# Decoder block with three-pass fp32 matmuls: the last three pairs of heads go batch by batch, with each batch's cross attention beside the next batch's steps

## The reference, cut to what matters

```python
# x (4,512,512), ctx (4,512,256); 16 heads = 8 pairs
x = layernorm(x + gated_slot_attention(x, Wq, Wk, Wv, Wg, Ws, Wo))   # per head: q,k,s 64 wide, v,g 128 wide
    # p = exp(s - cumlogsumexp(s)), a scan over tokens for keys, softmax over 64 slots,
    # a scan for values, rms norm, silu(g) gate, then @ Wo (the sum over heads)
# cross attention, per batch; logits are the x just normalised
q = ctx @ Wq.T + bq ; k = ctx @ Wk.T + bk
att = softmax(q @ k.T)                      # 512 x 512, one batch
x = layernorm(x + x @ att.T)
# FFN: BitNet (8-bit rows, ternary weights), Hadamard transform over the 2048 hidden values
gate, up = bitlinear(x, w_gate), bitlinear(x, w_up)
x = layernorm(x + bitlinear(hadamard(silu(gate) * up), w_down))
```

## Time and profile before

| | |
|---|---|
| median of 3 runs | 1638.67 us (1638.44 to 1642.08) |
| profiled execution, its time | 1641.68 us |
| its span, first to last instruction | 1639.8 us |
| mean granted PE clock | 0.976 of full speed |
| PE busy | 1536.7 us, 94% |
| DVE busy | 1038.5 us, 63% |
| ACT, POOL busy | 630.7 us, 367.8 us |

### The profile page before, as it was taken

One profiled execution on the slowest core, in us unless ns is written; L12 is line 12 of the kernel. 1 busy time (PEld: TensorE's weight loads), 2 busy tenths in 40 slices (PEclk: granted clock), 3 DMA queues, 4 the chain that ended last, 5 costly groups with the idle time before them and its releaser, 6 DMA issues.

```text
span 1639.8 us, 23987 instructions
## 1 busy us (share of the span) xinstructions
PE 1536.7 (94%) x9570; PEld 1215.1 (74%) x9570; DVE 1038.5 (63%) x1982; ACT 630.7 (38%) x1213; POOL 367.8 (22%) x246
## 2 busy tenths in 40 slices
PE   6999999999999999999999999896969797999986
PEld 5888888888888888888888888785746455656663
DVE  4566556556655655665565566465667777778785
ACT  4332333233233323323332332222132646567663
POOL 1111002001100202433342343232011333233210
PEclk9999999999999999999999999997989899999998
DMA  7111012111101200211121120210040122334451
GB/s 249 49 55 42 27 33 65 40 39 57 41 27 33 65 14 26 66 57 41 52 71 53 52 65 33 71 52 20 7 167 1 58 84 89 97 104 142 142 167 58
DMA packets 88062, 106.99 MB, mean 65 GB/s; under 512 B 4496, under 2 KB 58896, under 8 KB 87568
## 3 DMA queue, kind: packets, MB, share of 16 engines
q1 hardware_dynamic: 84496, 99.17, 18.8%
q10 hardware_dynamic: 3456, 6.29, 1.0%
HBM read 78.19 MB, written 27.26 MB: 64 GB/s over the span
## 4 chain that ended last, share of the span: by engine, by line
PE 85%; DVE 8%; issue 2%; ACT 2%; DMA 1%; POOL 1%; SPq 0%; POOLq 0%; DVEq 0%; ACTq 0%
PE bank L393 18%; PE bank L395 17%; PE bank L394 17%; PE bank L604 5%; PE bank L502 3%; PE bank L640 3%; PE bank L488 2%; PE bank L438 2%; PE bank L464 2%; PE bank L619 2%; PE bank L447 2%; PE bank L510 2%; PE bank L452 2%; PE bank L459 1%; PE bank L496 1%
## 5 line engine op out<-in xcount | busy, mean ns | idle before, releaser
L393 PE MATMUL bank<-Wh,X 128*128 128x512 f32 x512 | 211.2, 412 | 0.0
L395 PE MATMUL bank<-Wh,X 128*128 128x512 f32 x512 | 200.9, 392 | 0.0
L394 PE MATMUL bank<-Wl,X 128*128 128x512 f32 x512 | 200.1, 391 | 0.0
L731 ACT ACTIVATE V<-bank 128x256 f32<-128x256 f32 x128 | 49.2, 384 | 369.2 <-PE bank L395 369.2
L393 PE MATMUL bank<-X,Wh 128*128 128x512 f32 x384 | 163.6, 426 | 15.7 <-DVE X L905 13.0
L1287 POOL TENSOR_TENSOR sm<-sm,half 128x8 f32<-128x8 f32 x32 | 52.7, 1646 | 501.1 <-DVE sm L1010 501.1
L395 PE MATMUL bank<-X,Wl 128*128 128x512 f32 x384 | 153.2, 399 | 0.0
L394 PE MATMUL bank<-X,Wh 128*128 128x512 f32 x384 | 152.4, 397 | 0.0
L604 PE MATMUL bank<-XT,W 128*128 128x512 bf16 x512 | 123.2, 384 | 12.5 <-DVE M L1158 3.9
L1277 POOL TENSOR_SCALAR RAW<-RAW 128x1024 f32<-128x1024 f32 x24 | 87.4, 3640 | 158.3 <-ACT RAW L709 158.2
L953 DVE SCALAR_TENSOR_TENSOR U<-U,bank 128x256 f32<-128x256 f32 x128 | 51.7, 404 | 96.2 <-ACT U L733 96.0
(11 more groups left out here) (188 smaller groups left out, 3240.3 us busy)
## 6 DMA issues: line engine op xcount, KB each, us to landing
z_scratch<-EV SPq DMA_DIRECT2D x64, 256.0 KB, 2.0
Z<-z_scratch SPq DMA_DIRECT2D x16, 1024.0 KB, 6.0
RAW<-wgT SPq DMA_DIRECT2D x16, 512.0 KB, 3.8
RAW<-wuT SPq DMA_DIRECT2D x16, 512.0 KB, 3.7
RAW<-wdT SPq DMA_DIRECT2D x16, 512.0 KB, 3.6
w_scratch<-BW ACTq DMA_DIRECT2D x24, 256.0 KB, 2.0
W<-w_scratch SPq DMA_DIRECT2D x3, 2048.0 KB, 12.3
RAW<-Wo SPq DMA_DIRECT2D x8, 512.0 KB, 3.6
```

The source lines that it names most:

```text
L393: engine.matmul(o, lh(c), rh(c), start=c == 0, stop=False)
L394: engine.matmul(o, lh(c), rl(c), start=False, stop=False)
L395: last = engine.matmul(o, ll(c), rh(c), start=False, stop=c == n - 1)
L731: engine.activation(V[:, par, i, :], bk[:, 0:256], ACT.Copy).then_inc(S["v_evac"], 1)
```

## The change

The list of (pair, batch) is now a table, `PAIRS`. Pairs 0 to 4 go as before; pairs 5, 6 and 7 go batch by batch, with the pairs in turn up and down (5, 6, 7, then 7, 6, 5), so the last step of one batch and the first of the next share their weights. Batches end with steps 22, 25, 28 and 31. There are 14 sets of weights instead of 8. The new sets are loaded behind the last use before them, in loops 18, 19, 20, 22, 23, 25, 26, 28 and 29 for Q, K, S, VG (before: 18, 22 and 26 in that stretch).

The stages of cross attention are placed by four tables, one for each batch. `PLACED` are 16 stages of a loop, so place 16 n + i is behind the i-th of them in loop n; 496 on are the seam's 22 places, 518 on the units from 4. Batch 0 stands in loops 25 to 28 (all but `x_turned` in 25 to 27), batch 1 in loops 27 to 29, batch 2 from loop 29 to the seam; batch 3's softmax is in the seam, its `centre` at unit 4, its `xm0` at unit 16 and its `x_turned` at unit 29. Between values and unit 0 stands no `xm` any more, and `y` of step 31 moves behind unit 3.

The FFN's weight pieces (`tern`) may stand three times a loop, and all are made by loop 24. Buffers move: the low part of the context goes to the back half of `X1h`, low parts of the attention to two tiles of their own, `M` is in two pieces. `W3` (made weights) comes back in halves of columns: gate and up for units 0 to 7 first, then the rest, then the down weights. `x_turned_out` of batches 0 to 2 waits for other things that held its tile.

```diff
-WEIGHT = {"Q": 0, "K": 1, "S": 2, "VG": 4, "WO": 5}
+PAIRS = [(hp, b) for hp in range(5) for b in range(NB)]
+PAIRS += [(hp, b) for b in range(NB) for hp in ((5, 6, 7), (7, 6, 5))[b % 2]]
+FIRST = [n for n in range(STEPS) if n == 0 or PAIRS[n][0] != PAIRS[n - 1][0]]
+LOAD = [sum(f <= n for f in FIRST) - 1 for n in range(STEPS)]
+LAST = [f - 1 for f in FIRST[1:]] + [STEPS - 1]
+ENDS = [max(n for n in range(STEPS) if PAIRS[n][1] == b) for b in range(NB)]
...
+STEP = ("keys", "q", "scores", "states", "load_x", "k", "ok", "s", "tern", "turn_ok", "turn_o", "vg0", "tern",
+        "turn_w", "vg1", "y", "weights", "vg2", "values", "vg3", "tern")
+def step_order(n, tasks):
...
+        if stage == "tern":
+            terns += 1
+            if n and terns in ((2,) if n + 1 in LAST else (1, 2, 3)):
...
+def new_weights(stage, n):
+    l = LOAD[n]
+    if n != LAST[l] or l + 1 == LOADS:
+        return []
+    return {"q": [("Q", l + 1)], "k": [("K", l + 1)], "s": [("S", l + 1)], "y": [("WO", l + 1)],
+            "vg3": [("VG", l + 1, 0), ("VG", l + 1, 1)]}.get(stage, [])
...
-            if n == STEPS - 2 and stage in BETWEEN:
-                yield from cross_place(0, BETWEEN[stage])
+            if stage in PLACED and n > 20:
+                yield from beside(len(PLACED) * n + PLACED.index(stage))
+SEAM = (("keys", 31), ("scores", 31), ("states", 31), ("turn_o", 30), ("ok", 31), ("y", 30), ("turn_ok", 31), None,
+        ("turn_w", 31), None, None, None, ("weights", 31), ("values", 31), None, None, ("turn_o", 31), ("unit", 0),
+        ("unit", 1), ("unit", 2), ("unit", 3), ("y", 31))
+PLACES = (
+    dict(ctx=400, centre=403, n1=406, qk=406, qk_out=407, x101=411, x101_out=412, x123=416, x123_out=417,
...
+    dict(ctx=500, qk=502, qk_out=503, energy=506, energy_out=507, att_scale=508, att01=510, att01_out=511,
+         att23=511, att23_out=512, centre=518, n1=521, x101=524, x101_out=525, x123=527, x123_out=528, xm0=530,
...
-                if no == len(pieces) - 6:
-
-                    sp.wait_ge(S["proj_vg"], 4 * (STEPS - 3))
+                if loop >= 22 and 0 not in placed:
+                    sp.wait_ge(S["proj_vg"], 4 * ENDS[0] + 4)
                     engine.dma_start(XW[:, 0], xWqT.rearrange("(c p) n -> p c n", p=128)).then_inc(S["xw_in"], 16)
                     engine.dma_start(XW[:, 1], xWkT.rearrange("(c p) n -> p c n", p=128)).then_inc(S["xw_in"], 16)
                     context(0)
+                if loop >= 27 and 1 not in placed:
+                    sp.wait_ge(S["ctx_lo"], 1)
+                    context(1)
...
-            for k in range(3):
-                engine.dma_start(W3[:, k, :], scratch[k]).then_inc(S[f"w3_in{k}"], 16)
+            for h in range(2):
+                for k in range(2):
+                    v = lambda a: a.rearrange("p (c n) -> p c n", c=4)[:, :, 1024 * h:1024 * h + 1024]
+                    engine.dma_start(v(W3[:, k, :]), v(scratch[k])).then_inc(S[f"w3_in{h}"], 16)
+            sp.wait_ge(S["w_lo_g"], 6 * (LOADS - 1))
+            engine.dma_start(W3[:, 2, :], scratch[2]).then_inc(S["w3_in2"], 16)
```

More of the change, by code:

```diff
@@ L1 @@
+import math
 import numpy as np
@@ L37, in attention_order @@
+PLACED = [stage for stage in STEP if stage not in ("scores", "load_x", "tern")]
 def attention_order():
-    for stage in ("q", "k", "s", "vg0", "vg1", "vg2", "vg3"):
+    for stage in OF_NEXT:
         yield stage, 0
     yield "load_x", 2
-    tern = iter(range(51))
+    tasks = list(range(52))
     for n in range(STEPS - 1):
[L45 to L56, removed]
-            if n == STEPS - 2 and stage in BETWEEN:
-                yield from cross_place(0, BETWEEN[stage])
@@ L62 @@
-FIRST = {"weights": (("ctx", 0), ("centre", 0)), "values": (("n1", 0),), "vg3": (("qk", 0),)}
-BETWEEN = {"keys": 1, "q": 2, "states": 3, "k": 4, "ok": 5, "s": 6, "turn_o": 7, "vg0": 8, "turn_w": 9, "vg1": 10, "y": 11,
-           "weights": 12, "vg2": 13, "values": 14, "vg3": 15}
-def seam_order():
[L69 to L75, removed]
+        for stage, m in step_order(n, tasks):
+            yield stage, m
+            if stage in PLACED and n > 20:
+                yield from beside(len(PLACED) * n + PLACED.index(stage))
@@ L80, in seam_order @@
             yield item
[L84 to L101, removed]
@@ L106, with cross_places, beside @@
+CROSS = set(PLACES[0])
+def cross_places():
+    at = {}
+    for b in range(NB):
+        for stage, place in PLACES[b].items():
+            at.setdefault(place, []).append((stage, b))
+    return at
+BESIDE = cross_places()
+def beside(place):
+    return BESIDE.get(place, ())
 TILE = (("scale", 5), ("round", 6), ("clamp", 7), ("turn_q_out", 9), ("add", 11), ("normal", 12), ("store", 12),
         ("turn_q", 8), ("down", 10))
-SEAM_UNITS = 7
 LAG = 23
@@ L141 @@
         *(stage for stage, _ in TILE)}
[L144 to L167, removed]
 SEMAPHORES = """
-const_in gw_in raw0_in raw1_in am_in og_in v_in u_in y_in0 y_in1 y_in2 y_in3 ctx_in xw_in xb_in w3_in0 w3_in1 w3_in2 w3_store out_done
+const_in vec_in raw0_in raw1_in am_in og_in v_in u_in y_in0 y_in1 y_in2 y_in3 ctx_in xw_in w3_in0 w3_in1 w3_in2 w3_store out_done
 vec_made hk_zero
@@ L1336, in gpsimd @@
                     attend(stage, n)
+                    for key in new_weights(stage, n):
+                        w_low(key)
         def sync(engine):
@@ L1351, in sync @@
             held = {}
-            for no, (key, where) in enumerate(pieces):
+            placed = set()
+            for no, (key, where, loop) in enumerate(pieces):
                 if no == 10:
```

217 lines of the change are left out of this document (135 added, 82 removed).

## The result

The changed kernel takes 1585.62 us (median of 4 runs, 1584.94 to 1586.57) against 1639.16 of the kernel before in the same comparison. The ratio is 0.9671, with a 95% interval of 0.9654 to 0.9687: 53.5 us faster. Predicted were 1579.5 us and a range of 1556 to 1622. The profiled execution took 1585.25 us, its span is 1583.1.

What follows compares the result with a forecast made beforehand. PE was taken as the bound, losing 90.4 us late to waits and lower clock. 1549.6 without loss plus 1, 12 and 18 gave a 1580.6 us span, so 1579.5 us forecast; range 1556 to 1622.

Steps and rivals of the forecast that it cites:

- The reachable loss and its source: Loops 28 to 30, step 31 and the units: 90.4 us lost to late cross-attention stages or late loads; without loss 1549.6.
- The forecast case: Whole kernel: most lost time comes back, 1579.5 us, own range 1556 to 1606; chance 72%.
- Weights, 1 us: Loops 18 to 29: six more weight sets are covered by other work, costing 1 us; bounds 0 and 79.
- rival 3: Nine loops with a weight set: slots starve PE, 8.8 us each, 1659 us, slower by 19; chance 5%.
- The late FFN piece, 8.8 us: Loop 28: no FFN piece is fetched there any more, so its 8.8 us loss is gone.
- Loops 25 to 30, 12 us: Cross attention of batches 0 to 2 beside the loops loses 2 us a loop, 12 in all; bounds 0 and 66.
- Step 31, 10 us: Step 31: DVE decides, with a root on POOL as last link before unit 0; 10 us lost.
- Units 0 to 22, 8 us: Units 0 to 22: 8 us lost for the start and for centre and n1 between h and gs.
- The signs: Trace readings named beforehand, such as step 31's keys at 1205 to 1220 us; wrong if loops 28 to 30 exceed 52.
- 1: Step 31 and the units: waits stay, 59.7 us lost as before, 1622 us (1621 as median); chance 10%.
- 2: Loops 25 to 30: DVE and POOL queues jam, batches 0 to 2 lose 21.9 us each, 1634 us; chance 10%.
- 4: Whole kernel: no effect, through mishaps that happen to sum to 60 us; chance 3%.

Runs made afterwards that it cites:

- Run 1: Changed kernel with the last pairs in order 5, 6, 7 for every batch: 17 weight sets instead of 14, last FFN pieces two loops later; 1587.24 us.
- Run 2: Kernel before, with SP's loads of the context and its weights three FFN pieces later; 1630.73 us, ratio 0.9945.
- run 8: Changed kernel without POOL's root of the attention output's mean square, so values differ; 1579.66 us against 1585.97 for the changed kernel on the same chip.
- a11_scale: Also run 11: a10_early with batch 0's scaling of exponentiated rows one place earlier on DVE, ahead of an instruction waiting for PE; 1580.63 us.
- run 6: Changed kernel with the splits of batch 3's context (ACT, POOL) one place earlier, 499 instead of 500; 1586.38 us.
- run 3: Changed kernel with batch 0's cross attention packed on places 426 to 444 instead of 400 to 444; 1597.38 us.
- a4_ring0: Changed kernel with batch 0's second x1 and its energy two places later and the halves of its att one place later; 1583.01 us.
- a9_norecip: Changed kernel with DVE's reciprocal of the running sums replaced by a short copy, so values differ; 1581.66 us, ratio 0.9644.
- a10_early: a4_ring0 with batch 0's row maxima on DVE one place earlier, ahead of DVE's step for ok; 1582.53 us, ratio 0.9652.

## Why the prediction was right

**The reachable loss and its source: right.** The end without any loss was put at 1549.6 us. The span came out 33.5 above it, where 31 were predicted. Of the 6.1 us between 1579.5 and 1585.62 the span makes 2.5; 3.4 come from taking off 3.0 us because the profiled execution of before was above its median, while the one of after is 0.4 under its own. The tail reads 86.98 us against 87.2. (The mark at 1552.60 that the prediction calls unit 63 is in fact unit 62's, so the stretch before it holds 39 units and its own loss was 5.1 us, not 2.0; the same mark is 1496.12 after, and what the prediction kept of it was the same 5.1, so its total stands. The forecast case's 1556 to 1606 also means 7.5 to 57.5 us of loss by the prediction's own sum, not 10 to 56.)

**Weights, 1 us: right.** Loops 18 to 24 take 35.8 to 36.1 us with a set in five of them. Loop 22, where the context goes ahead of Q, took 0.2 more. No `ok` waits for HK. Run 1 prices a set at some 0.5 us, where rival 3 needed 6.7 a loop. Loop 25 starts at 924.19 us, 1.1 earlier than laid out.

**The late FFN piece, 8.8 us: right.** Run 2 took it away alone and gained 9.2.

**Loops 25 to 30, 12 us: mis-sized, 21.9 measured.** "2 us a loop" was the term: the losses aren't even. Loops 25 and 29 lose nothing with 32.5 and 36.1 us of DVE, loop 26 loses 6.3 with 30.9. I had set DVE's share of a loop against PE's and looked for a full engine. What is lost is PE arriving at the end of a chain over several queues (C): runs 8 and 11 took that away with DVE's work the same, and loop 26 came down to its content. DVE held 30.9 to 38.9 us in a loop, no more than the 35 to 42 put down. The waits of PE in these loops add up to 14.6 us. The granted clock of 0.97 in loops 26, 28 and 30 makes some 5 of the other 7 (an estimate: 3% of 50.25, 56.36 and 53.31 us).

**Step 31, 10 us: near, 13.5 measured.** It takes 45.49 us with DVE busy 39.94, where I had 36. The waits are 2.48 for the context, 2.0 for `OKN`, 1.0 for `XI` and 3.2 for `OG`, 8.7 together; the granted clock of 0.92 makes some 3.6 more (an estimate: 8% of 45.49). The root on POOL that I named as the last link is there, but it is that of `OG` ahead of `turn_o`, and run 8 shortened this wait by 1.7. "Here DVE decides" is right in so far as DVE's largest values set the end of the wait for `OKN` (run 6). What less work on DVE in this step alone would give wasn't tried.

**Units 0 to 22, 8 us: too much, 2.0 measured.** 70.95 us instead of 126.39. With only batch 3's second half beside it the start of the FFN costs next to nothing. The stretch from unit 23 to the mark of unit 62 took 160.12 us where 162.6 were laid out, and no part of the prediction says why. So 9.9 us too few in the loops and 3.5 in step 31 met 6.0 too many in units 0 to 22, 2.5 in the stretch behind them and 2.1 up to loop 25 (the 1 for the weights and the 1.1 above): that the span came within 2.5 us is partly luck.

**The signs.** Step 31's `keys` at 1219.56 us is inside 1205 to 1220. Unit 0 at 1265.05 and unit 23 at 1336.00 are later than the 1255 and the 1320 to 1335 that were forecast. Loops 28 and 30 are above 52 us, one half of a sign of being wrong, but DVE is busy for 68 and 73% of them, not over nine tenths.

**The rivals.** 1 needed 59.7 lost in step 31 and the units; 15.5 were. 2 needed 66 in the loops; a third of it was there, and run 3 shows its mechanism for one batch with less room: 11.8 us. 3 fell by run 1, 4 by the result itself.

## What to carry to other kernels

Before saying that an engine beside the bottleneck is too full, follow one wait back through all queues: in a loop with that engine a third idle, letting eight ready instructions pass one that waited gave back 4.7 us, of which the wait itself was 2.96. Work that is spread beside a full engine gives its price back only if its stages have room for their latency; moving one stage moves its PSUM bank too, and the wait shows up at whoever takes that bank next, so change one batch at a time and read the waits again. Price a waiting loop by its content, not by its neighbours' average.

## What the runs showed of the hardware

**A wait of some 2 us cost PE either nothing more or 1.7 us more.** In loop 28 PE waits for `OG` and then does the same transposes in the changed kernel and in a4_ring0, here one below the other:

```profile
1066.74 1.15 PE L619 MATMUL bank<-IDB,XI 128*128 128x128 bf16 x16 [2.04 <-DVE OG L1058]
1067.69 2.02 PE L625 MATMUL bank<-C,ax 128*128 128x128 f32 x8
```

```profile
1065.92 1.07 PE L619 MATMUL bank<-IDB,XI 128*128 128x128 bf16 x16 [2.00 <-DVE OG L1058]
1066.82 1.11 PE L625 MATMUL bank<-C,ax 128*128 128x128 f32 x8
```

After 2.04 us idle the eight matmuls took 2.02 us and the granted clock of the loop was 0.97 (2.4 GHz, with a stretch at 1.2); after 2.00 us idle they took 1.11 and the loop ran at 1.00. The loops took 56.36 and 54.69 us. In a9_norecip the wait was 2.24 us and in a10_early 2.05, and neither cost anything more (54.51 and 54.72 us); in a11_scale it was 2.04 and cost it again (56.38). Loop 26 shows the same: waits of 1.7 and 2.8 us in the changed kernel and in a9_norecip, but 50.25 us at 0.97 in the one and 48.74 at 1.00 in the other. So the lower clock doesn't come after each wait, as the prediction has it, the length of the wait alone doesn't decide, and an edit in another loop can tip it. What does decide wasn't tried, and gains of 1 to 2 us in these runs can't be read without the granted clock beside them. It is why a4_ring0's loop 28 gained though nothing in it had moved, and why 1.7 of a11_scale's 4.7 us went again (54.72 in a10_early, 56.38).

**A multiply on DVE waited out a subtraction on POOL.** In the timeline of a10_early one of four equal multiplies took 1.51 us instead of 0.49, from 983.23 to 984.74. POOL at that time:

```profile
983.19 1.26 POOL L1316 TENSOR_TENSOR Wl<-RAW,Wh 128x512 fp32r<-128x512 f32 x1 [6.84 <-ACT Wh L721]
```

It ended at 984.45, and the multiply 0.29 later. In the changed kernel the worst of the 32 normalising multiplies rose from 1601 to 2604 ns, with the median at 540:

```profile
L1089 DVE TENSOR_SCALAR Y<-Y,mv,rs x32: 533/540/2604, 940.2 to 1347.3; 128x512 f32<-128x512 f32 x32
```

The rule of the Trainium skill that the prediction weighed ("SBUF — State Buffer", "Who interferes with whom": VectorE in a two-port mode and GpSimd lock a shared port pair for a whole instruction) says the same, and the trace agrees, though no row shows which mode the multiplies are in: in the changed kernel's cross attention the four groups of normalising and scaling multiplies with a long one in them each stand beside a subtraction on POOL (L1316 or L1357). The long ones cost DVE some 6 us in all (an estimate, from the groups' 2.97, 3.97 and 3.46 us where four such multiplies take 1.91, and one scaling multiply of 1.48 for 0.49).
